# Linear attention and a top-2 mixture of experts on one core: one rounding, the order of the weight splits and the place of a row turn are changed

## The reference, cut to what matters

```python
def ffn(x, W1, b1, W2, b2, Wr, br):              # x is the normalized xn
    logits = xf @ Wr + br
    topv, _ = lax.top_k(logits, 2)
    masked = jnp.where(logits >= topv[:, 1:2], logits, -jnp.inf)
    weights = jax.nn.softmax(masked, axis=-1)
    h = jax.nn.gelu(jnp.einsum('td,edh->eth', xf, W1) + b1[:, None, :], approximate=False)
    expert_out = jnp.einsum('eth,ehd->etd', h, W2) + b2[:, None, :]
    return jnp.einsum('etd,te->td', expert_out, weights)
out = x + attention(xn) + ffn(xn)
```

## Time and profile before

| | |
|---|---|
| median of three runs | 712.09 us |
| the profiled execution | 712.84 us |
| its span on the core | 710.4 us |
| mean granted TensorE clock | 0.994 |
| busy: PE, DVE, ACT, POOL | 685.6, 514.4, 476.1, 227.6 us |
| bytes moved by DMA | 91.65 MB, 129 GB/s on average |

### The profile page before, as it was taken

One profiled execution on the slowest core, in us unless ns is written; L12 is line 12 of the kernel. 1 busy time (PEld: TensorE's weight loads), 2 busy tenths in 40 slices (PEclk: granted clock), 3 DMA queues, 4 the chain that ended last, 5 costly groups with the idle time before them and its releaser, 6 DMA issues.

```text
span 710.4 us, 17625 instructions
## 1 busy us (share of the span) xinstructions
PE 685.6 (96%) x5482; PEld 602.7 (85%) x5483; DVE 514.4 (72%) x1306; ACT 476.1 (67%) x875; POOL 227.6 (32%) x169
## 2 busy tenths in 40 slices
PE   8899999999999998999999999999999999999995
PEld 4666777777777776499999999999999999999995
DVE  8889989898989878857657675556767444577553
ACT  5687969696969786785477764456775444677551
POOL 1313232323242415623252322234223323323322
PEclk9999999999999999999999999999999999999998
DMA  8766474747474647756455563345636333544432
GB/s 261 194 181 168 107 224 105 224 104 230 99 232 98 201 106 226 224 166 189 63 98 171 73 164 47 54 66 87 182 57 169 55 49 63 88 132 75 60 46 23
DMA packets 87205, 91.65 MB, mean 129 GB/s; under 512 B 60049, under 2 KB 73361, under 8 KB 84897
## 3 DMA queue, kind: packets, MB, share of 16 engines
q1 hardware_dynamic: 71426, 59.36, 33.6%
q0 software_dynamic: 13872, 18.75, 15.0%
q10 hardware_dynamic: 1872, 13.11, 5.1%
HBM read 39.32 MB, written 26.67 MB: 93 GB/s over the span
## 4 chain that ended last, share of the span: by engine, by line
PE 74%; DVE 11%; issue 6%; ACT 5%; SPq 1%; DMA 1%; ACTq 0%; POOL 0%; POOLq 0%; DVEq 0%
PE F L501 8%; PE F L503 7%; PE F L502 7%; PE WK L501 4%; PE WK L503 4%; PE WK L502 4%; PE DEN L575 4%; PE F L563 4%; PE NUM L501 4%; PE NUM L503 3%; PE NUM L502 3%; PE DEN L503 3%; PE DEN L501 3%; PE DEN L502 3%; PE F L557 3%
## 5 line engine op out<-in xcount | busy, mean ns | idle before, releaser
L1869 POOL DMA_INDIRECT out<-ysb,icur x75 | 120.4, 1606 | 278.2 <-DVE ysb L1700 262.3
L1167 ACT ACTIVATE h<-F,b1c 128x384 f32<-128x384 f32 x200 | 112.2, 575 | 143.9 <-PE F L503 135.7
L1677 DVE TENSOR_TENSOR hl<-h,hh 128x768 fp32r<-128x768 f32 x100 | 96.2, 963 | 121.5 <-ACT hh L1171 121.5
L1021 ACT ACTIVATE e_ring<-F 128x512 f32<-128x512 f32 x256 | 145.4, 621 | 36.3 <-PE F L557 32.9
L501 PE MATMUL F<-gxh,wh 128*128 128x384 f32 (+1 forms) x400 | 129.0, 323 | 2.3 <-DVE gxl L1457 1.4
L503 PE MATMUL F<-gxh,wl 128*128 128x384 f32 (+1 forms) x400 | 128.0, 320 | 0.0
L502 PE MATMUL F<-gxl,wh 128*128 128x384 f32 (+1 forms) x400 | 128.0, 320 | 0.0
L1803 POOL DMA_INDIRECT xg<-rows,slots x64 | 63.6, 994 | 175.7 <-PE F L557 143.1
L1411 DVE SCALAR_TENSOR_TENSOR kp<-F,e_ring 128x512 f32<-128x512 f32 x128 | 82.5, 680 | 10.7 <-PE DEN L575 6.2
L1411 DVE SCALAR_TENSOR_TENSOR qp<-F,e_ring 128x512 f32<-128x512 f32 x128 | 84.8, 682 | 4.8 <-ACT e_ring L1021 3.6
L1171 ACT ACTIVATE hh<-h 128x768 fp32r<-128x768 f32 x100 | 84.7, 847 | 3.3
(11 more groups left out here) (250 smaller groups left out, 1561.1 us busy)
## 6 DMA issues: line engine op xcount, KB each, us to landing
wraw<-experts ACTq DMA_DIRECT2D x12, 1024.0 KB, 6.6
gblk<-xg SPq DMA_DIRECT2D x100, 96.0 KB
Sk<-kdh SPq DMA_DIRECT2D x64, 128.0 KB, 2.4
Sq<-qdh SPq DMA_DIRECT2D x64, 128.0 KB
xin<-x SPq DMA_DIRECT2D x8, 512.0 KB
Sk<-kdl SPq DMA_DIRECT2D x32, 128.0 KB, 2.4
Sq<-qdl SPq DMA_DIRECT2D x32, 128.0 KB
xres<-x SPq DMA_DIRECT2D x8, 512.0 KB
```

The lines of the kernel that those rows point to most:

```text
L1021: A(e_ring[:, u % 4, :], F[u % 4][:, :], ACT.Exp, bias=EXP_BIAS, scale=1.0 / DOWN).then_inc(exp_done, 1)
L1167: A(h32[:, m, :], F[m % 4][:, 0:T], ACT.Gelu, bias=b1c[:, w, m:m + 1]).then_inc(gelu, 1)
L1677: V.tensor_tensor(hl[:, 2 * q:2 * q + 2, :], h32[:, 2 * q:2 * q + 2, :], f32(hh[:, 2 * q:2 * q + 2, :]), ALU.subtract).then_inc(hl_rdy, 1)
L1869: pool.indirect_dma_start(out, bass.IndirectOffsetOnAxis(icur[:, s, :], 0), ysb[:, s, :], None, bounds_check=last_token, compute_op=ALU.ad ...
```

## The change

1. `hidden` on ACT no longer makes the rounding of the last pair (`q` = 3); `hidden_lo` on DVE makes it with a `tensor_copy` of the same 768 columns, in front of its subtraction.
2. In `finish` the four `weights_lo` stand ahead of `row_targets` and `rows_tokens`.
3. `load_rows` requests the four square DMAs when the previous squares have been turned (`gx_turned`), and only the fifth, `gtok`, waits for `grow_free`. In front of tile 1 the copies of `first_rows_tokens` now count on `gx_turned`.
4. In tile 0 DVE's `turn_rows(1)` moves from behind the first two outputs to between the third and the fourth `hidden_lo`, and `rows_lo(1)` behind the fourth. ACT's `rows_hi(1)` moves in front of the four `weights_hi`.

```diff
@@ -443,11 +443,12 @@
 
         def load_rows(g, first):
 
-            sp.wait_ge(grow_free, g + 1)
+            sp.wait_ge(gx_turned, g)
             tile = xg[bass.ds(first, T), :]
             for i in range(4):
                 sp.dma_start(gblk[32 * i:32 * i + 32, :, :, :].rearrange("b j k a -> b j (k a)"),
                              tile[:, 64 * i:64 * i + 64].rearrange("(j b) c -> b j c", b=32)).then_inc(grow_ld, 16)
+            sp.wait_ge(grow_free, g)
             sp.dma_start(gtok[:, :, :],
                          tile[:, W_COL:W_COL + E + 8].rearrange("(s p) c -> p s c", p=P)).then_inc(grow_ld, 16)
 
@@ -1050,7 +1051,7 @@
 
         def rows_hi(g):
 
-            act.wait_ge(gx_turned, g)
+            act.wait_ge(gx_turned, g + 1)
             for k in range(KT):
                 A(gxh[:, k, :].rearrange("p (j b) -> p j b", b=32), gx32[:, :, k, :], ACT.Copy).then_inc(gxh_rdy, 1)
 
@@ -1167,8 +1168,9 @@
                 A(h32[:, m, :], F[m % 4][:, 0:T], ACT.Gelu, bias=b1c[:, w, m:m + 1]).then_inc(gelu, 1)
             if q == 0:
                 act.wait_ge(y_full, SUB * g + SUB)
-            act.wait_ge(gelu, 4 + MT * g + 2 * q + 2)
-            A(hh[:, 2 * q:2 * q + 2, :], h32[:, 2 * q:2 * q + 2, :], ACT.Copy).then_inc(hh_rdy, 1)
+            if q < MT // 2 - 1:
+                act.wait_ge(gelu, 4 + MT * g + 2 * q + 2)
+                A(hh[:, 2 * q:2 * q + 2, :], h32[:, 2 * q:2 * q + 2, :], ACT.Copy).then_inc(hh_rdy, 1)
 
         def tile(g, e, w, next_weights=False):
             act.wait_ge(w_rdy, e + 1)
@@ -1192,10 +1194,10 @@
         for g in range(2):
             at_lo(NB - 1, g)
         hidden(0, 0, 3)
+        rows_hi(1)
         for c in range(PIECES):
             weights_hi(1, 1, c)
         end_0 = act.value_load(counts_i[0:1, 1, 1:2], min_val=1, max_val=E * TT)
-        rows_hi(1)
         act.wait_ge(o_rdy, 2 * NB + 2)
         act.dma_start(out_rows[NB - 1], o_sb[:, :, :]).then_inc(row_st, 16)
         load_raw = load_raw_on(act)
@@ -1442,7 +1444,7 @@
         def first_rows_tokens():
 
             V.tensor_copy(wnext[:, :, :], grow[:, :, W_COL:W_COL + E])
-            V.tensor_copy(inext[:, :], grow[:, :, TOK_COL]).then_inc(grow_free, 1)
+            V.tensor_copy(inext[:, :], grow[:, :, TOK_COL]).then_inc(gx_turned, 1)
 
         def turn_rows(g):
 
@@ -1673,6 +1675,10 @@
 
 
         def hidden_lo(g, q):
+
+            if q == MT // 2 - 1:
+                dve.wait_ge(gelu, 4 + MT * g + MT)
+                V.tensor_copy(hh[:, 2 * q:2 * q + 2, :], h32[:, 2 * q:2 * q + 2, :]).then_inc(hh_rdy, 1)
             dve.wait_ge(hh_rdy, 4 * g + q + 1)
             V.tensor_tensor(hl[:, 2 * q:2 * q + 2, :], h32[:, 2 * q:2 * q + 2, :],
                             f32(hh[:, 2 * q:2 * q + 2, :]), ALU.subtract).then_inc(hl_rdy, 1)
@@ -1703,11 +1709,11 @@
         def finish(g, e, t, w, next_weights):
 
             rows_lo(g + 1)
-            row_targets(g, e, t)
-            rows_tokens(g + 1)
             if next_weights:
                 for c in range(PIECES):
                     weights_lo(e + 1, 1 - w, c)
+            row_targets(g, e, t)
+            rows_tokens(g + 1)
             biases(g, e)
             for s in range(SUB):
                 outputs(g, e, s)
@@ -1729,7 +1735,9 @@
             products(NB - 1, n)
         hidden_lo(0, 1)
         hidden_lo(0, 2)
+        turn_rows(1)
         hidden_lo(0, 3)
+        rows_lo(1)
         for i in range(2):
             residual(NB - 1, i, PROJ_LAST)
         for c in range(PIECES // 2):
@@ -1740,8 +1748,6 @@
         biases(0, 0)
         outputs(0, 0, 0)
         outputs(0, 0, 1)
-        turn_rows(1)
-        rows_lo(1)
         rows_tokens(1)
         weights_lo(1, 1, 2)
         outputs(0, 0, 2)
```

## The result

The changed kernel takes 718.91 us (median of four runs, 717.75 to 719.60), the kernel before 712.09 us. The ratio is 1.0091, 95% interval 1.0079 to 1.0103: slower by 6.8 us, outside the range of the prediction. The profiled execution took 718.33 us with a span of 716.2, against 712.84 and 710.4 before. Lines of kernel.py have moved by 1 to 6: `mm3` is L502 to L504, the subtraction L1683, DVE's rounding L1681, the turn L1452.

A forecast was written before the change was run, and what follows sets the result against it. PE, busy 96% of the span, was taken as the bound, so only its waits could be won. The terms +0.95 - 0.46 - 0.07 - 0.76 = -0.34 us took the median of 712.09 to 711.7 us, range 710.1 to 713.8.

The forecast's parts named there:

- (c) of part 2: After an expert's first tile: targets, token copies and outputs end as before, and later `gtok` still precedes the turn; cost nothing.
- (b): ACT's weight requests: the next tile's GELU starts earlier, two short tiles' `hl` waits fall from 0.80 to 0.42; 0.76 us gained.
- Part 4: Tile 0: the earlier turn waits for squares landing at 316.9, PE stands 2.4 us; net cost +0.95 us.
- Rival B: Tile 0, PE's new stop from 317.3 to 319.5: the granted clock falls, price 1.7 us, total 713.4 us; chance 0.20.
- Part 1: Fourth pair: DVE's copy takes 0.55 us and brings the fourth `hl` 0.35 us forward; the five 0.42 us waits stay.
- seven-wait argument: PE's `hl` waits in the expert stage: PE waits for the third pair, so the fourth rounding leaves seven waits.
- Part 2 (a): PE before the last two experts' first tiles: earlier `wl` gains 0.46 us at 633.38 and 0.07 before 650.79.
- Part 3: Loop tiles: earlier square requests win nothing, since DVE never waits for `gblk` there; 0, at worst a few tenths.
- Rival A: Tile 0: the squares land at 315.8 or sooner in most executions; total 710.6 us at 315.8, 709.9 at 315.1; chance 0.27.
- C: Expert stage: relieving ACT of a quarter of its roundings removes the `hl` waits, 5.5 us more, 706.2 us; chance 0.04.
- D: Expert stage: fourth rounding does nothing, as the turn's wait or `wh` pieces decide `w_rdy`; two gains halve, 712.4 us; chance 0.09.

The follow-up runs named there:

- own-semaphore run: Changed kernel, but `gtok` counts on a semaphore of its own, so the turn waits for the four square DMAs alone; ratio 0.9974 to the kernel before.
- half-load run: Changed kernel, but the second `wraw` DMA of experts 1 to 7 loads 128 columns in place of 2048; ratio 0.9951 to the kernel before.
- part 1 alone: Kernel before, with only the fourth rounding moved from ACT to DVE; ratio 0.9974 to the kernel before.
- first experiment: The same as the own-semaphore run: changed kernel with `gtok` on its own semaphore; ratio 0.9974 to the kernel before.

## Why the prediction was wrong

**The step that failed** is (c) of part 2: "The copies free `gtok` 4.7 us later, so its DMA lands about 3 us into the next tile, and the next turn comes at about 6. Cover enough; without it DVE would stand at the turn." The later request and the consequence were named; what was wrong is the landing. About 3 us into the tile is what follows if `gtok` takes what it took in the kernel before, 2.3 to 2.9 us in the loop tiles. It landed 8.3 us into the tile, at 391.9, 8.4 us after its request. The turn was wanted at 389.45, 5.9 into the tile, so the cover that (c) counted on was there, and the landing was 2.44 us too late for it. The step stood in the sum as nothing; in its place the two short tiles took 4.60 and 1.80 us more, and the 0.76 of (b) was lost in them. Without its failure, in the own-semaphore run, the ratio of 0.9974 comes to 710.2 us, inside the range of the prediction. Two lines above, under (b), the same text had the 2 MB request of ACT move forward, released by the same last subtraction. The two moves were never laid on one time axis: against the start of the tile on PE, `wraw`'s request came forward by 0.85 us (from +0.30 to -0.55) and `gtok`'s went back by 2.41 (from -2.53 to -0.12), and they passed each other. (The request went back by 2.41 and not 4.7, since before it had stood behind the four squares' requests on SP.) The half-load run (0.9951), where `gtok` lands in 5.7 us, and the own-semaphore run (0.9974), where it is late and the turn does not wait for it, show it from both sides.

**The order of the transfers in tile 0 had been read, and not carried over.** Part 4 of the prediction found the squares behind 2 MB of `wraw` in the same queue and put their landing at 316.9, some 6 us after the last of the requests. At 383 the 2 MB are in another engine's queue, and there the question was not asked; the trace shows that this did not protect `gtok`.

**Rival B, the clock,** was named for another place. The granted clock fell with the stop of 2.86 us before 393.76 and cost about 2.5 us there, and in a second execution it fell after tile 0's stop as well, where the stretch took 1.46 us more. The price in the prediction was 1.7 us; that longer stops would come elsewhere was missing.

**What held.** Part 1: the copy was 0.557 us each (0.55 predicted), and PE's waits for the third pair stayed. The seven-wait argument is shown by part 1 alone (still seven waits) and supported by its reverse, the run in which DVE takes the second rounding and turns later. Part 2 (a): 0.53 predicted, 0.60 measured (17.41 to 17.05 and 17.41 to 17.17). (b): 0.76 predicted; two tiles of 12.19 and 12.20 in the own-semaphore run, 0.77. Part 3: nothing, measured 1.0001; but that with part 2 beside it most of the damage hangs on it was not seen. Part 4: +0.95 predicted, +0.72 measured. DVE at tile 0 of the kernel after:

```profile
315.83 0.98 DVE L1452 STREAM_TRANSPOSE gx<-gblk 128x768 f32<-128x768 f32 x1 [5.28 <-DMA gtok<-xg]
316.73 0.52 DVE L1681 CAST hh<-h 128x768 fp32r<-128x768 f32 x1
317.28 0.96 DVE L1683 TENSOR_TENSOR hl<-h,hh 128x768 fp32r<-128x768 f32 x1
318.16 1.02 DVE L1459 TENSOR_TENSOR gxl<-gx,gxh 128x384 fp32r<-128x384 f32 x2
```

The turn waits 5.28 us and starts at 315.83, with tile 0 starting 0.95 earlier: 316.8 on the old axis, where the prediction had 316.95. Rounding and subtraction follow, `hl` is there at 318.2, PE at 318.39 after 2.00 idle. That the landing was met to 0.2 us is partly luck: the prediction gave 316.9 to the squares, but the turn waited for `gtok` too, and without it (first experiment) starts 16.92 us after tile 0, at 316.15 on the old axis. Rival A (squares at 315.8 or sooner) did not come about; C and D neither.

## What to carry to other kernels

When an edit moves a step, move its DMA requests on the time axis as well, and do the same for every other request whose trigger the edit moves: two small shifts can change which transfer is in front, and a large transfer requested just behind a small one still delayed it here. A wait that counts several DMAs on one semaphore is as late as the least important of them, so a small transfer that is needed later should have its own. And before work is moved from one engine to another, find which of the repeated steps the waiting engine waits for: the fourth of four equal roundings was worth 1.7 us by the medians, of which the trace shows 1.0; the second in its place, together with the later turn, another 4.4.

## What the runs showed of the hardware

24 KB in 64-byte packets took 1.8 to 2.9 us from issue to landing on their own. They took 8.4 us when another engine's queue had been given 1 MB 0.43 us earlier and another MB 0.10 us later, and 5.7 us when this second MB was all but left out. A queue of its own did not shield them: no packet of theirs moved for 3.6 us. Why the DMA engines served them so late is open.

The granted clock fell to 0.50, from 392.8 to 399.6, with a stop of PE of 2.86 us between dense work, but not after 2.61 us in the same execution, and in the run without part 1 not after 2.93 us at the same place. In the second execution of the changed kernel it fell with both of these tiles' stops (2.90 and 3.33 us), and after the 1.98 us of tile 0, where it had stayed at 1.00 after 2.00 us in the first. The Trainium skill (TensorE: Matmul & The Clock Gate, Part 1) says that the gate follows recent activity; the trace agrees, and shows that an equal stop is punished in one execution and not in another.

The first four times of the changed kernel spread over 1.9 us, those of the kernel before over 0.5. Side by side later it was 6.0 (717.17 to 723.20) and 3.0 (711.13 to 714.17). That the clock makes the difference is shown for two profiled executions only, by the 3 us above.
